# A compressed-interaction tower: the second layer a unit at a time, in column quarters, from the fifth tile on, and a reordered head

## The reference

```
e  = stack of tbl_f[ids[:, f]]                        # b x 32 x 32
x0 = e
for W in (W0, W1):                                    # 1024 x 128 and 4096 x 128
    z  = einsum('bhd,bmd->bhmd', e, x).reshape(b, -1, 32)
    x  = einsum('bpd,pj->bjd', z, W)
    res.append(x)
z = concat(res).sum(over d)                           # b x 256
h = relu(concat(z, dense_ctx) @ W_top1 + b_top1)      # 272 -> 512
h = relu(h @ W_top2 + b_top2)                         # 512 -> 256
y = h @ W_top3                                        # 256 -> 1
```

## Time and profile before

| | us |
|---|---|
| median of the runs | 361.77 (361.23 to 362.09) |
| the profiled execution | 362.34 |
| its span | 360.5 |
| PE busy, PEld busy | 321.7, 299.3 |
| ACT, DVE, POOL busy | 242.9, 198.0, 246.0 |
| mean granted clock of PE, as a share of 2.4 GHz | 0.976 |
| chain that ended last, by engine | PE 58%, POOL 16%, ACT 9%, issue 8%, DVE 6% |

### The profile page before, as it was taken

One profiled execution on the slowest core, in us unless ns is written; L12 is line 12 of the kernel. 1 busy time (PEld: TensorE's weight loads), 2 busy tenths in 40 slices (PEclk: granted clock), 3 DMA queues, 4 the chain that ended last, 5 costly groups with the idle time before them and its releaser, 6 DMA issues.

```text
span 360.5 us, 11477 instructions
## 1 busy us (share of the span) xinstructions
PE 321.7 (89%) x4680; PEld 299.3 (83%) x4680; DVE 198.0 (55%) x702; ACT 242.9 (67%) x774; POOL 246.0 (68%) x262
## 2 busy tenths in 40 slices
PE   1999918767879989998999899989997999899997
PEld 1887817566779989998999899989987889899897
DVE  4348989676055555555654665566455545455301
ACT  1588744965558697768776876787687666767702
POOL 5777777777777777777777777777777777772000
PEclk9999976999699999999999999999999999999999
DMA  7901000000011000111001100101011010000000
GB/s 226 324 16 17 13 14 16 15 13 15 15 16 16 15 16 16 17 15 15 15 16 16 16 15 16 16 16 18 15 15 16 15 16 15 16 16 7 3 2 0
DMA packets 10772, 9.78 MB, mean 27 GB/s; under 512 B 4664, under 2 KB 8896, under 8 KB 10720
## 3 DMA queue, kind: packets, MB, share of 16 engines
q0 software_dynamic: 8192, 4.21, 7.9%
q1 hardware_dynamic: 2528, 4.84, 3.9%
HBM read 9.03 MB, written 0.00 MB: 25 GB/s over the span
## 4 chain that ended last, share of the span: by engine, by line
PE 58%; POOL 16%; ACT 9%; issue 8%; DVE 6%; DMA 2%; SPq 0%; DVEq 0%; ACTq 0%
PE WA L857 19%; POOL emb L317 16%; PE PA L812 11%; PE QB L826 6%; DVE RT L482 4%; PE PA L767 3%; PE QB L772 3%; ACT TS L324 3%; PE M L870 3%; ACT eblk L324 3%; PE T L840 2%; PE M L889 2%; PE M L880 2%; DMA TS<-in_W 1%; PE ET L799 1%
## 5 line engine op out<-in xcount | busy, mean ns | idle before, releaser
L317 POOL DMA_INDIRECT emb<-in_table,rows x256 | 245.3, 958 | 80.4 <-issue 77.4
L704 DVE COPY TS<-T 32x64 f32<-32x64 f32 x256 | 55.4, 217 | 92.4 <-PE T L840 85.4
L812 PE MATMUL PA<-eblk,zP 128*128 128x132 f32 x512 | 74.7, 291 | 2.0 <-issue 1.2
L812 PEld LDWEIGHTS PA<-eblk,zP 128*128 128x128 f32 x512 | 65.5, 198 | 9.3 <-issue 6.5
L324 ACT ACTIVATE TS<-T 32x64 f32<-32x64 f32 (+1 forms) x320 | 66.5, 208 | 7.8
L857 PE MATMUL WA<-TS,RT 128*128 128x128 f32 x512 | 61.0, 275 | 0.3 <-ACT TS L324 0.3
L324 ACT ACTIVATE TS<-PA 128x396 f32<-128x396 f32 (+1 forms) x96 | 43.4, 464 | 26.3 <-PE PA L812 25.8
L857 PEld LDWEIGHTS WA<-TS,RT 128*128 128x128 f32 x512 | 59.0, 192 | 0.6 <-ACT TS L324 0.6
L324 ACT ACTIVATE eblk<-eT 32x256 f32<-32x256 f32 x128 | 53.5, 418 | 3.1
L667 DVE TENSOR_TENSOR zP<-ET,eT 128x512 f32<-128x512 f32 x32 | 22.1, 692 | 32.7 <-ACT eT L324 32.4
L678 DVE TENSOR_TENSOR zQ<-ET,eT 128x1024 f32<-128x1024 f32 x32 | 38.9, 1215 | 0.0
(11 more groups left out here) (91 smaller groups left out, 366.7 us busy)
## 6 DMA issues: line engine op xcount, KB each, us to landing
emb<-in_table,rows POOLq DMA_INDIRECT x256, 2.4
TS<-in_W SPq DMA_DIRECT2D x8, 256.0 KB, 5.3
wt<-in_W_top SPq DMA_DIRECT2D x2, 512.0 KB, 8.6
y1w<-in_W_rows SPq DMA_DIRECT2D x1, 448.0 KB, 6.8
TS<-in_W_rows SPq DMA_DIRECT2D x1, 448.0 KB, 8.4
sym<-in_W_cols SPq DMA_DIRECT2D x1, 264.0 KB, 2.7
TS<-in_W_cols SPq DMA_DIRECT2D x1, 264.0 KB, 3.0
idc<-in_ids SPq DMA_DIRECT2D x1, 128.0 KB, 2.0
```

The lines of the kernel that those rows point to most:

```text
L317: eng.indirect_dma_start(emb[par][:, g, :], None, table, bass.IndirectOffsetOnAxis(rows[:, k, g:g + 1], 0))\
L704: eng.tensor_copy(view(ts[32 * q:32 * q + 32, :, :], P * REST + b0, [[4 * P, 2], [P, 4], [1, 8]]), view(src, q, [[C17, 2], [4, 4], [C33, 8 ...
L812: m = eng.matmul(PA[t % 2][:, NQ * C33 * x:NQ * C33 * x + NQ * C33].rearrange("p (v c) -> p v c", c=C33), zP[u % 2][:, g, :], eblk[u % 2][ ...
```

## The change

1. `S0 = 4`, `WIDE = 16`: tiles 0 to 3 keep `second` and `first`. `second(3)` stands whole in unit 16, `first(3)` in unit 19. For units 16 to 31 there is `narrow(v, part)`: the unit's 32 columns of a `TS` slot are the weights and the 128 columns of C are moved. Product n goes to the quarter n % 4 of the 128 output partitions, so that a quarter holds a fourth of the sum. Part 0 (48 products) stands at the start of unit v+1; part 1 (8 products, and 7 of the first layer in the two other quarters) behind T3's products.
2. The four quarters are added and turned back by `select(v)`: ACT (`s_copy`, partitions 64 to 127, 256 columns) and DVE (`s_half`, partitions 0 to 63, 128 columns) copy the bank to `S`, PE multiplies `S` with `sel` (four 32x32 identities on top of one another), two products of 32 columns, and ACT (`n_copy`) copies both layers' results to 32 columns of `zf`, which becomes two buffers.
3. The tower of tile k stands in units 4k+7 to 4k+9 as before, that of tile 6 in units 29 to 31. `last_tile` does `narrow` of units 30 and 31 and the tower, its dense part (`wt1d`) first.
4. Head: of units 0 and 1 ACT copies three of T3's four row groups (`by_vector` is 1). `high_sums` is cut in two, its second half behind unit 1's copies; `early_sums` loses three of its sums to `low_sums` and `cross_sums`, which are later. `eblk_copy` of unit 2 and `e_copy` of unit 3 move. The 14 weight groups stand singly: ahead of the triples (`C_FRONT`), after two blocks (`C_MID`) or at the unit's end (`C_END`).

```diff
+        S0 = 4
+        WIDE = UNITS * S0
+        L1_AT = {4 * k + 7: k for k in range(TILES - 2)} | {ALL - 3: END - 1}
+        L2_AT = {u + 1: k for u, k in L1_AT.items()}
+        Y_AT = {u + 2: k for u, k in L1_AT.items()}
...
-        FIRST_UNIT = ((), (), (), (0, 1, 2, 3), (4, 5, 6, 7), (8, 9, 10, 11), (12, 13), ())
+        C_FRONT = {3: (0, 1), 5: (6,), 6: (9, 10), 7: (13,)}
+        C_MID = {3: (2,), 4: (4,), 5: (7,), 6: (11,)}
+        C_END = {3: (3,), 4: (5,), 5: (8,), 6: (12,)}
...
         def by_vector(u):
-            return 2
+            return 1 if u < 2 else 2
...
+            def s_copy(v):
+                n = v - WIDE
+                eng.wait_ge(s_made, n + 1)
+                wait(eng, n_made, n - 1)
+                copy(S[n % 2][64:P, :], narrow_bank(v)[64:P, 0:2 * P]).then_inc(s_kept, 1)
+
+            def n_copy(v):
+                k, unit = divmod(v, UNITS)
+                eng.wait_ge(n_made, v - WIDE + 1)
+                wait(eng, l1_made, k - 1)
+                copy(zf[k % 2][:, :, 32 * unit:32 * unit + 32],
+                     narrow_bank(v)[:, 2 * P:2 * P + 64].rearrange("p (c b) -> p c b", b=32)).then_inc(n_kept, 1)
...
                 part_copy(TRIOS * u)
                 part_copy(TRIOS * u + 1)
+                for n in C_MID.get(u, ()):
+                    c_copy(n)
                 across_copy(u)
+                if WIDE < u < ALL - 1:
+                    s_copy(u - 1)
                 part_copy(TRIOS * u + 2)
+                if WIDE < u < ALL - 1:
+                    n_copy(u - 1)
...
-            high_sums()
+            high_sums(0)
             rest_copies(0, 0)
-            rest_copies(0, 1)
             all_products(2)
             rest_copies(1, 0)
-            rest_copies(1, 1)
+            high_sums(1)
             all_products(3)
...
+            def narrow(v, part):
+                k, unit = divmod(v, UNITS)
+                bank, cols = narrow_bank(v), slice(32 * unit, 32 * unit + 32)
+                ts = TS[k % 2]
+                if part == 0:
+                    eng.wait_ge(p_kept, TRIOS * (v + 1))
+                    eng.wait_ge(q_kept, 2 * (v + 1))
+                    if v == ALL - 1:
+                        eng.wait_ge(z_made, NZ * ALL)
+                    elif v == WIDE:
+                        eng.wait_ge(y2_kept, S0)
+                    else:
+                        eng.wait_ge(n_kept, v - WIDE)
+                else:
+                    eng.wait_ge(t3_kept, kept_before(v + 1))
+                    eng.wait_ge(t3_also, also_before(v + 1))
+                if part == 0:
+                    for n in range(F + HALF):
+                        j, kt = n % NQ, KT_ORDER[n]
+                        eng.matmul(bank[32 * j:32 * j + 32, 0:P], ts[:, slot_of(kt), cols], c_slot(kt),
+                                   start=(n < NQ), stop=(j >= 2 and n >= F + HALF - NQ))
+                    return
+                for x in range(KT - F - HALF):
+                    kt, j = KT_ORDER[F + HALF + x], x % 2
+                    if x < Y1T:
+                        eng.matmul(bank[64 + 32 * j:96 + 32 * j, P:2 * P], ts[:, Y1_SLOTS[x], cols], y1w[:, x, :],
+                                   start=(x < 2), stop=(x >= Y1T - 2))
+                    m = eng.matmul(bank[32 * j:32 * j + 32, 0:P], ts[:, slot_of(kt), cols], c_slot(kt),
+                                   start=False, stop=(x >= KT - F - HALF - 2))
+                m.then_inc(s_made, 1)
+
+            def select(v):
+                n = v - WIDE
+                eng.wait_ge(sel_made, NQ + 2)
+                eng.wait_ge(s_kept, n + 1)
+                eng.wait_ge(s_also, n + 1)
+                for c in range(2):
+                    m = eng.matmul(narrow_bank(v)[:, 2 * P + 32 * c:2 * P + 32 * c + 32], S[n % 2][:, P * (1 - c):P * (2 - c)], sel[:, :],
+                                   start=True, stop=True)
+                m.then_inc(n_made, 1)
...
             def last_tile():
-                second(END, 0, 24)
-                result(END - 1)
-                second(END, 24, F + HALF)
-                first(END)
-                second(END, F + HALF, KT)
...
+                narrow(ALL - 2, 1)
+                eng.wait_ge(p_kept, TOTAL - 1)
+                eng.wait_ge(q_kept, 2 * ALL)
+                for a in (0, 2, 3):
+                    eng.matmul(L1_BANKS[a], wt1d[:, P * a:P * a + P], dT[:, P * END:P * END + P], start=True, stop=False)
+                narrow(ALL - 1, 0)
+                narrow(ALL - 1, 1)
+                select(ALL - 2)
+                eng.matmul(L1_BANKS[1], wt1d[:, P:2 * P], dT[:, P * END:P * END + P], start=True, stop=False)
+                select(ALL - 1)
+                eng.wait_ge(n_kept, ALL - WIDE)
...
             for u in range(ALL):
                 fill(u)
                 triples(TRIOS * u)
                 triples(TRIOS * u + 1)
+                for n in C_MID.get(u, ()):
+                    weights(n)
                 across_triples(u)
                 other_triples(u)
+                if WIDE < u < ALL - 1:
+                    narrow(u - 1, 1)
                 triples(TRIOS * u + 2)
-                if UNITS < u < ALL - 1 and u % UNITS == UNITS - 1:
-                    hidden1(u // UNITS - 1)
+                if WIDE < u < ALL - 1:
+                    select(u - 1)
+                for n in C_END.get(u, ()):
+                    weights(n)
+                if u in L1_AT:
+                    hidden1(L1_AT[u])
                 if ahead(u) is not None:
                     emb_transposes(ahead(u))
```

More of the change, by code:

```diff
@@ L123, in dlrm_cin_tower @@
         TH = sb("TH", [P, F, THIRD])
-        zf = sb("zf", [P, 2, P])
+        zf = [sb(f"zf{i}", [P, 2, P]) for i in range(2)]
+        sel = sb("sel", [P, 32])
+        S = [sb(f"S{i}", [P, 2 * P]) for i in range(2)]
         h1 = sb("h1", [P, N1, P])
@@ L188, in dlrm_cin_tower @@
         y1_kept = sem("y1_kept")
+        sel_made = sem("sel_made")
+        s_made = sem("s_made")
+        s_kept = sem("s_kept")
+        s_also = sem("s_also")
+        n_made = sem("n_made")
+        n_kept = sem("n_kept")
         l1_made = sem("l1_made")
@@ L236, in pieces @@
                 return (0, 16, 28, 44, KT)
-            if k == END - 1:
-                return (0, 18, 38, KT, KT)
             return (0, 9, 22, 41, KT)
@@ L615, in early_sums, with high_sums, cross_sums @@
                 both_across(0, 0, SUB, False, early_first)
[L616 to L619, removed]
+                apart_across(1, 0, 0, HALF, False, low_first)
+                eng.wait_ge(early_first, 8)
                 both_across(0, 0, SUB, True, high_added)
[L621 to L632, removed]
+                cross_first(0, 0, SUB, cross_made)
+            def high_sums(part):
+                if part == 0:
+                    eng.wait_ge(rt_kept, F)
+                    eng.wait_ge(rx_kept, F // 2)
+                    own_firsts(1)
+                    own_seconds(1)
+                if part == 1:
+                    both_across(0, SUB, SUB, False, high_first)
+                    eng.wait_ge(high_first, 8)
+                    both_across(0, SUB, SUB, True, high_added)
             def low_sums():
                 apart_across(1, 1, 0, HALF, False, low_first)
+                eng.wait_ge(low_first, 2 * 5)
+                for e in range(2):
+                    apart_across(1, e, 0, HALF, True, low_added)
+            def cross_sums():
                 cross_first(0, SUB, SUB, cross_made)
[L638 to L643, removed]
+                cross_first(1, 0, HALF, cross_made)
+                eng.wait_ge(cross_made, 3)
+                for c0 in (0, SUB):
+                    cross_second(0, c0, SUB, cross_added)
                 cross_second(1, 0, HALF, cross_added)
@@ L698, in rest_copies @@
                     if unit == 0:
-                        wait(eng, y2_made, k - 1)
-                        wait(eng, y1_made, k - 1)
+                        ts_free(eng, k)
                 b0 = 32 * unit + 8 * j
@@ L748, in _ @@
                     rest_sums()
-            for j in range(by_vector(ALL - 1)):
-                rest_copies(ALL - 1, j)
+                if u == 2 * UNITS:
+                    eng.wait_ge(const_s, 2)
+                    for j in range(NQ):
+                        eng.tensor_copy(sel[32 * j:32 * j + 32, :], ident[32 * j:32 * j + 32, 32 * j:32 * j + 32]).then_inc(sel_made, 1)
+                    for i in range(2):
+                        eng.memset(S[i][0:64, P:2 * P], 0.0).then_inc(sel_made, 1)
+                if WIDE < u:
+                    if u == ALL - 1:
+                        for j in range(by_vector(u)):
+                            rest_copies(u, j)
+                    s_half(u - 1)
+            s_half(ALL - 1)
             eng.wait_ge(tower_loaded, 16 * 5)
@@ L936, in fill @@
                 k, i = divmod(u, UNITS)
[L937 to L941, removed]
+                if u in Y_AT:
```

(26 more changed lines are left out.)

97 lines of the change are left out of this document (55 added, 42 removed).

## The result

The kernel after takes 371.25 us (median of 4, 369.77 to 372.57), the kernel before beside it 361.93 (361.23 to 364.25): ratio 1.0258 [1.0224, 1.0291]. The forecast was 359.7, with a range up to 365.5. In the profiled executions the span grew from 360.5 to 369.5, 9.0 us.

A forecast was written before the change was run, and what follows sets the result against it. PE was taken to bind until about unit 26, then the gathers. The lump spends the head's 10.6; unit 31's transposes come 6.9 later, the tail saves 9.0: 361.77 - 2.1 = 359.7 us, range 353.5 to 365.5.

The forecast's parts named there:

- The head: Up to unit 16: unit 8 opens 13 us earlier, of which 10.6 can be kept; unit 16 opens at 180.8.
- The waits of units 4 to 7: PE's waits once weight groups stand singly: 1.4, 2.5, 2.0 and 1.1 us in units 4, 5, 6 and 7.
- the floor: Unit 15's opening: its gathered rows are not there before 169.4, 3.0 after the last gather's issue.
- The rival that the head gives less: Units before 16: less than 10.6 gained, two to four us lost if the clock falls; 361 to 363, chance 0.13.
- The lump: Unit 16 does all of second(3), 112 instructions in 12.5, and lasts 18.1 us; unit 17's transposes at 198.9.
- The narrow unit: Units 17 to 30: a plain unit takes 8.2 us with both narrow parts, select and hand-offs; fourteen take 114.7.
- the rival of open weight loads: Narrow products: each group of four waits for its weight loads, 3.5 us a unit; about 410, chance 0.03.
- the round-trip rival: select behind s_copy, part 0 behind n_copy: copies end later or select costs 0.45; unit 8.4 to 8.6, 363 to 365, chance 0.23.
- Other work in units 17 to 30: first(3) 1.56, four hidden1 9.7, four hidden2 7.2 and four result 4.5, together 22.9 us.
- The gathers to the end: Rival: at 7.7 us a unit PE catches up with the gathers, unit 31 opens at 329.3; 352.5, chance 0.14.
- The tail: From unit 31's transposes to the span's end: 21.9 us in place of 30.9, 9.0 saved.
- Outside the span: Device time beyond the span: the profiled execution's difference (362.34 with its 360.5 span, 0.57 over the median) carries over.

The follow-up runs named there:

- e1: The kernel after with second(3) in unit 16 called in three parts (32, 16 and 8 slots), each asking only for its own slots: 364.04 us, ratio to before 1.0048.
- e2: The kernel after with 26 products that nobody reads (52 instructions) ahead of second(3) in unit 16, its wait kept: 368.62 us, ratio to before 1.0168.
- e7: e1 with select's four instructions done twice: 370.05 us, ratio to before 1.0211.
- e5: e1 with result behind part 0 of narrow instead of ahead of it in units 17, 21, 25, 29 and 31: 359.43 us, ratio to before 0.9928.
- e4: e1 with the old head (weight groups, by_vector, place of copies and order of sums of the kernel before): 374.42 us, ratio to before 1.0336.
- e3: The kernel before with the new head alone (copies, sums, single weights), second layer and end as before: 361.92 us, ratio to before 1.0002.
- e8: e1 with S0 = 6, so tiles 4 and 5 go wide and narrow starts at unit 24: 365.20 us, ratio to before 1.0084.

## Why the prediction was wrong, step by step

- **The head: right in size, with single terms off.** Units 4 and 8 opened at 64.18 and 106.88 (64.3 and 107.9), and unit 16 at 180.03 (180.8). T of unit 1 came at 47.07 (47.8 for 54.40):

```profile
47.07 0.66 PE L905 MATMUL T<-eblk,z 128*32 128x132 f32 x16 [1.51 <-ACT TS L350]
```

The waits of units 4 to 7, counted as 7.0, show as 4.6 in the brackets. The sum has no clock in it, and the clock did fall, to 0.60 in 48 to 52 and 0.55 in 52 to 56, without costing the head its gain; the stretch at 90 to 99, at 0.62 before, now ran at 1.00. Unit 15 waited for its gather as foretold but opened at 168.61, where the floor was 169.4: its last gather was issued at 166.16 and its rows were there 2.45 later, for the 3.0 read off unit 27. The rival that the head gives less is out.
- **"The lump": this step failed.** It said: "Unit 16 now does all of `second(3)`: 112 instructions at 0.1117 ... 12.5 ... 18.1 us. Unit 17's transposes: 198.9." The instructions were priced right (18 in 2.00 is 0.1111 and not 0.1117, which is 0.07 over 112): in e1, where nothing stands ahead of them, the unit takes 18.06 and unit 17 opens at 198.32. What the step left out is the call's wait. Before, the piece in the first unit behind a tile needs only PA's slots, and the one that needs T's stands three units later; one call from 0 to 56 asks for everything at its start, ACT's last copy of unit 15 included, and those copies stand behind nine other instructions on ACT. I costed what PE issues and never asked what its first instruction waits for, although two other steps (`select`, part 0) were worked out just so. The sentence that "eblk, T copies and `part_copy` still end before PE asks for them" was about narrow units; in unit 16 the T copies end at 185.93, and in e1 PE is ready for the first product at 180.48. 5.66 of wait, shown by e1, and 2.96 of lower clock behind it, shown by e2, make 8.6 of the 8.75. The clock too was a term at nothing: the prediction gave a fall of the clock a price in the head alone.
- **The narrow unit: right but for one term.** 8.34 for 8.19, within the 8.0 to 8.35 that I gave myself, at its very edge. Groups of four follow every 0.109 (64 instructions in 1.74), so the rival of open weight loads, 410, is out. (Its price of 0.11 a load of T's is the mean of all 512, 112 ns; the earlier trace rows shows only four merged, 0.13.) `select` cost 0.44 for 0.30: I had chosen between 0.11 and 0.45, and the upper end was the truth, which e7 confirms. The wait of part 0 is 0.15 (0.2), and of `select` nothing is seen to wait. By the round-trip rival's own price for `select` (0.45) it half came true: 14 x 0.15 = 2.1 is the gain that I had forecast, and e1, with the lump mended, is at 1.0048: slower than before.
- **Other work in units 17 to 30:** 140.5 less 14 x 8.34 is 23.7 for 22.9. `result` waits 0.91 at unit 17, as it did:

```profile
208.17 0.71 PE L1010 MATMUL M<-h,wt 128*128 128x128 f32 x4 [0.91 <-ACT h L446]
```

I took that wait over as it was; e5 shows that it needn't be there.
- **The gathers to the end: out.** In the kernel after PE waits for them twice, 2.2 in all, and not once behind unit 16.
- **The tail: right.** 22.1 from unit 31's transposes to the end (21.9, before 30.9); `last_tile` behind L1035 takes 4.8 as before.
- **Outside the span: mis-sized, cause open.** I carried over 1.3, a median time (361.77) less the span of another execution (360.5). Execution by execution, time less span is 1.76 to 1.88 in 23 of the kernel before, 1.77 to 3.07 in four of the kernel after and 1.76 to 3.50 in twelve of e1, with a median of 2.56; e4 and e5 are raised too, the other kernels are like before. No run says why. Of the 4.3 by which e1's median misses the forecast, 2.5 lie in its profiled span (338.83 + 22.1 for 336.5 + 21.9), and the rest outside it and between executions.

## What to carry to other kernels

When pieces of a loop are joined in one call, the call's first instruction inherits the waits of all pieces: list for each wait when its last producer, in its own queue's order, is done, and keep the pieces apart where one comes late. A stand of PE is to be priced with what the clock does behind it, from a window over the instructions that follow. And an early gain is worth what the slowest stage behind it lets through: the same head gave 0 us here before a stage that waits for gathers, and 10.4 where PE stays behind the gathers to the end, so ask first who binds after it.

## What the runs showed of the hardware

- After PE had stood 5.66 us the granted clock was 0.50 from 186 to 190 and 0.73 on average from 190 to 194; 64 instructions took 10.11. With 52 unread instructions in the same time it stayed 1.00, and the 64 took 7.22.
- PE waited 2.45 for a gather in e3, and the granted clock was 0.72 from 250 to 256; in e8, after 0.16, it was 1.00 in the same window of the same unit.
- An fp32 instruction with 128 weight columns and only 32 moving columns took 0.111 (eight in 0.89, e7), as long as one with 128 moving columns (0.1116). In column quarters, 32 weight columns and 128 moving, four instructions together took 0.109.
